# Shared-network products from fp32r parts in the mixing stage of a three-stage transformer kernel

## The chip, the cores and the metric

The kernel runs on one core of a Trainium2 chip. The metric is device time in microseconds of one execution of the whole program. A core has five engines with programs of their own that wait for each other through semaphores: TensorE (PE in the profile), VectorE (DVE), ScalarE (ACT), GpSimd (POOL) and SyncE (SP, which issues DMAs). Each engine executes its program strictly in the order in which it is written.

## The reference

Eight sequences of 512 tokens and 256 features go through attention, then each gets one class row in front (513 rows), then a linear recurrence and a mixture of experts:

```
h = attention(x)                                  # 16 heads
h = concat([cls, h], axis=1)                      # 513 rows a sequence
u = layernorm(h)
h = h + (C @ scan(Bu)) + D * u                    # state h_t = W h_{t-1} + B u_t, W circulant
u2 = layernorm(h)
shared = (silu(u2 @ Wg_s.T) * (u2 @ Wu_s.T)) @ Wd_s.T
probs = sigmoid(u2 @ Wr.T + rb); top 2 of 8 experts
out = h + shared + sum over the 2 experts of score * expert(u2)
```

Everything is fp32 at the interface.

## The kernel before

The program has four stages, each a block that ends for all engines together: the projections of q, k and v (`stage_qkv`), the attention (`stage_attention`), the mixing (`stage_mix`) and the experts (`stage_experts`). The change is in the mixing, with some placing of buffers in `program`.

The mixing goes through the eight batches (sequences) one after the other as a software pipeline written out by hand: every engine has a function `step(b, par, prev, this, nxt)`, called for b = 0 to 8. In step b an engine works on batch b (`this`), finishes the shared network of batch b - 1 (`prev`) and prepares batch b + 1 (`nxt`). Steps 1 to 6 run in a loop. There is no planner: the order of the lines is the order of the work.

TensorE's step: transposes of the normalised rows u (L1028); block 1 of the shared network of batch b - 1 (`shared_up`, L1058; a block m is a quarter of the 512 hidden features, its gate half and its up half); the product with m1 that makes the recurrence's input (L1096); block 2; transposes of the next attention heads; block 3; a small count for the experts' places (L1077, L1079); the product of the recurrence's result with m2 (L1040, `by_token`); the down products of batch b - 1 (L1066); transposes of u2; the output projection of batch b + 1 (L1040 too); the router's logits (L1127); block 0 of batch b. The operands of all of these are fp32.

VectorE's step: the choice of two experts for batch b - 1 (`top_two`, L733 to L742, and L1244); gate times up of blocks 0 and 1 (`shared_act`, L1186); then, when m1's product is made, four rotations (L1260 to L1263), two scans (L1264, L1266) and six operations to turn back (L1270 to L1276); gate times up of blocks 2 and 3; the rows' places in the experts' table (`place`, L1225 to L1231); sum and statistics of h2 (L1200 to L1208); normalising to u2 (L1214); the adds of the down products (L1191); sum and statistics of the next h (`first_sum`); the router's bias (L1313); normalising the next u. In step 0 there is also the work on the class rows (L1357 to L1370).

ScalarE copies transposes from PSUM (L963), computes the silu of each block (L959) and the sigmoid (L1002), and in steps 7 and 8 rounds expert weights to fp32r (`shorten_weights`, L770), which VectorE then subtracts from the weights to have the second part (`cut_weights`, L778).

GpSimd computes u times d and adds h (L909, L915), the power -1/2 of the variances (L903, `inverse_deviation`) and issues for each batch eight indirect DMAs that scatter row numbers and scores to the table (L930). SyncE loads the heads, stores u2 and h2, and loads one expert's weights a batch.

The expert stage already multiplies from two fp32r parts of both operands, through `split_products` (L72): short times short, short times rest, rest times short. An fp32 matmul of 128x512 shows as two records in the trace, an fp32r one as one.

## Time and profile before

| | us |
|---|---|
| median of 3 runs | 1290.72 |
| lowest, highest | 1283.68, 1291.52 |
| profiled execution | 1272.49 |
| its span | 1270.7 |
| its mean TensorE clock | 0.969 of full |
| PE busy in the span | 1168.8 (92%) |
| DVE busy | 828.0 (65%) |
| ACT busy | 496.1 (39%) |
| POOL busy | 394.5 (31%) |
| 600 to 700 us: PE, DVE, ACT, POOL busy | 95.39, 79.21, 22.55, 41.39 |

The profile is of one execution, so sums of durations stand against 1272.49, and the runs' median is 18 us above it. The stretch from 600 to 700 us lies wholly in the mixing stage, which begins at about 523 us with the class rows; its last down products run at 856 us, and the expert stage's first transposes start at 881.1. Busy shares do not say what an engine waits for; that is read from the waits and from the engines' instructions in order of time.

### The profile page before, as it was taken

To read this page: it belongs to the slowest core of one execution; us is meant where nothing else is said; L and a number is where in the kernel's file an instruction comes from. 1 tells how busy PE (TensorE), PEld (TensorE's weight loads), DVE (VectorE), ACT (ScalarE), POOL (GpSimd) and SP (SyncE) were. 2 spreads that over 40 slices of the span, in tenths; PEclk is the share of its full clock that TensorE was granted. 3 is DMA by queue.
4 is the path that set the end of the run, shared out by engine and by line. 5 is a ranking of instruction groups with operands and counts; after the bars stand their busy time and mean duration, and the time that the engine had idled before them with its cause. 6 is when DMAs were issued, how large, how long until landed. Compare 5 with 4: busy or idle time off the path is not lost. (4 is left out here: it accounts for less than half of the span.)

```text
span 1270.7 us, 21184 instructions
## 1 busy us (share of the span) xinstructions
PE 1168.8 (92%) x5606; PEld 699.3 (55%) x5607; DVE 828.0 (65%) x1463; ACT 496.1 (39%) x867; POOL 394.5 (31%) x515
## 2 busy tenths in 40 slices
PE   6996999999999999759999999982999999999997
PEld 3552233333333332445566665552888888888885
DVE  4998888888888885278777788884343333333432
ACT  2430677777777777421212121440222222222221
POOL 1021441011110111022443333452355544455543
PEclk9996899999999999889999999996999999999999
DMA  8885223333333321203444223311233333333332
GB/s 287 307 272 194 71 89 108 96 93 101 105 90 96 109 85 56 83 1 84 100 99 97 73 48 80 83 34 34 34 50 50 53 53 52 50 50 50 52 55 35
DMA packets 108675, 113.05 MB, mean 89 GB/s; under 512 B 26080, under 2 KB 97904, under 8 KB 107600
## 3 DMA queue, kind: packets, MB, share of 16 engines
q1 hardware_dynamic: 90528, 89.05, 24.4%
q0 software_dynamic: 18112, 23.57, 10.7%
q8 instruction: 17, 0.28, 0.1%
q14 instruction: 18, 0.15, 0.0%
HBM read 68.81 MB, written 43.62 MB: 88 GB/s over the span
## 5 line engine op out<-in xcount | busy, mean ns | idle before, releaser
L637 DVE TENSOR_REDUCE neg_max<-by_query 128x2 f32<-128x1024 f32 x256 | 301.7, 1220 | 62.8 <-PE by_query L538 62.1
L696 ACT ACTIVATE k_wu_e<-by_key 128x512 f32<-128x512 f32 x512 | 277.2, 601 | 83.5 <-PE by_key L546 80.1
L546 PE MATMUL by_key<-k_wg_e 99*128 99x512 bf16 x512 | 180.2, 386 | 2.6 <-ACT k_wu_e L696 2.1
L1455 POOL DMA_INDIRECT out_rows<-y,k_slot x72 | 113.9, 1583 | 189.8 <-DVE y L1583 175.2
L538 PE MATMUL by_query<-k_wg_e 96*128 96x512 bf16 x512 | 161.3, 398 | 11.6 <-PEq L106 7.5
L1543 ACT ACTIVATE gate<-ps_up 128x512 f32<-128x512 f32 x72 | 43.0, 598 | 321.8 <-PE ps_up L72 321.8
L1504 PE MATMUL ps_y<-k_wd_e,acts_T 128*128 x576 | 136.0, 379 | 0.8 <-ACT acts_T L1552 0.8
L557 PE MATMUL pv<-k_wu_e,k_wd_e 128*32 128x512 f32 x1024 | 136.2, 604 | 0.2 <-ACT k_wu_e L696 0.2
L72 PE MATMUL ps_up<-w_short,x_T 128*128 x288 | 133.5, 464 | 0.4 <-issue 0.4
L546 PEld LDWEIGHTS by_key<-k_wg_e 99*128 99x128 bf16 x512 | 42.1, 97 | 144.5 <-ACT k_wu_e L696 84.8
L1504 PEld LDWEIGHTS ps_y<-k_wd_e,acts_T 128*128 128x128 f32 x576 | 109.0, 189 | 18.0 <-issue 1.0
L72 PE MATMUL ps_up<-w_short,x_rest 128*128 x288 | 113.8, 395 | 0.0
L1567 DVE CAST x_T<-ps_x 128x256 fp32r<-128x256 f32 x72 | 30.6, 425 | 104.2 <-PE ps_x L1477 104.2
L538 PEld LDWEIGHTS by_query<-k_wg_e 96*128 96x128 bf16 x512 | 47.6, 100 | 85.6 <-DVE k_wd_e L651 13.2
L451 POOL CAST k_max_parts<-neg_max 128x16 bf16<-128x16 f32 x32 | 6.1, 190 | 283.7 <-PE by_key L546 244.9
L1583 DVE TENSOR_SCALAR y<-ps_y,k_slot 128x256 f32<-128x256 f32 x72 | 34.8, 484 | 77.9 <-DMA out_rows<-y,k_slot 64.1
L791 POOL DMA_INDIRECT k_x_in<-kept_x_rows,k_slot x72 | 70.7, 982 | 28.7 <-issue 21.1
L1576 DVE TENSOR_TENSOR acts<-gate,ps_up 128x512 f32<-128x512 f32 x72 | 49.6, 688 | 46.1 <-PE ps_up L72 46.1
L930 POOL DMA_INDIRECT kept_table<-k_pay,k_slot_i x64 | 67.1, 1049 | 23.5 <-issue 18.4
L206 PE MATMUL qk_ps<-k_wu_e,k_wqkv 128*128 128x512 f32 x128 | 57.8, 605 | 12.2 <-DMA k_wu_e<-in_xT 12.2
L903 POOL TENSOR_TENSOR mix_rstd<-mix_mv,k_minus_half 128x4 f32<-128x4 f32 x16 | 16.4, 1026 | 149.3 <-DVE mix_mv L1208 149.2
L1058 PE MATMUL mix_pairs<-k_mix_u_T,k_wg_s 128*128 128x512 f32 x128 | 61.3, 602 | 0.7 <-DVE mix_act_T L1186 0.6
(204 smaller groups left out, 1764.1 us busy)
## 6 DMA issues: line engine op xcount, KB each, us to landing
k_wg_e<-kept_qk SPq DMA_DIRECT2D x384, 64.0 KB, 2.1
kept_qk<-qk_parts SPq DMA_DIRECT2D x32, 384.0 KB, 3.4
kept_v<-v_ones SPq DMA_DIRECT2D x8, 1024.0 KB, 5.8
k_wd_e<-kept_v SPq DMA_DIRECT2D x32, 256.0 KB, 3.0
k_wu_e<-in_xT POOLq DMA_DIRECT2D x8, 512.0 KB, 4.4
kept_heads<-k_wd_e SPq DMA_DIRECT2D x8, 512.0 KB, 3.0
k_heads_in<-kept_heads SPq DMA_DIRECT2D x8, 512.0 KB, 11.3
k_wg_e<-in_wg_e SPq DMA_DIRECT2D x8, 512.0 KB, 6.7
```

The source lines that it names most:

```text
L72: mm = pe.matmul(out, short(lhs[a]), short(rhs[b]), start=(start and n == 0), stop=(stop and n == 2))
L206: mm = pe.matmul(qk_ps[:, j, :], wqkv[:, c, j * P:(j + 1) * P], xt[:, par, c, :], start=(c == 0), stop=(c == DC - 1))
L538: pe.matmul(by_query[:, pair_bank(b, g, k // 2) + k % 2, :], q_rows[0:KROWS, g, h, t * P:(t + 1) * P], k_rows[0:KROWS, g, h, :], start=Tru ...
L546: pe.matmul(by_key[:, key_bank(job), :], k_rows[0:SROWS, g, h, kt * P:(kt + 1) * P], q_rows[0:SROWS, g, h, :], start=True, stop=True).then ...
L557: mm = pe.matmul(pv[VW * h:VW * (h + 1), :], v_unit[:, g, kt, h, :], probs[:, G * (kt // 2) + h, kt % 2, :], start=(kt == 0), stop=(kt == ...
L637: dve.tensor_reduce(neg_max[:, g % 2, 2 * n:2 * n + 2], by_query[:, bank:bank + 2, :], AX.X, ALU.max, negate=True).then_inc(query_read, 1)
L696: act.activation(probs[:, key_tile(j) // 2 * G + j // 2 % G, j % 2, :], by_key[:, key_bank(job), :], ACT.Exp, scale=float(HD) ** -0.5).the ...
L791: pool.indirect_dma_start(out=mem["x_in"][:, r % FIRST_X, :], out_offset=None, in_=dram["x_rows"], in_offset=bass.IndirectOffsetOnAxis(ap= ...
L930: pool.indirect_dma_start(out=dram["table"], in_offset=None, in_=mem["pay"][:, t, n, :], out_offset=bass.IndirectOffsetOnAxis(ap=mem["slot ...
L1058: mm = pe.matmul(pairs[:, m % 2, n, :], w[:, c, m * P:(m + 1) * P], u2_T[:, c, :], start=(c == 0), stop=(c == DC - 1))
L1455: pool.indirect_dma_start(out=dram["out"], in_=y[:, r % 2, :], in_offset=None, compute_op=ALU.add, out_offset=bass.IndirectOffsetOnAxis(ap ...
L1504: mm = pe.matmul(ps_y[:, r % 2, 0:D], acts_T[:, m, :], mem["wd_e"][:, bass.ds(e, 1), m, :], start=(m == 0), stop=(m == FC - 1))
```

## The change

`shared_up` takes its products from two fp32r parts of the weights and of u2, three fp32r matmuls in place of one fp32. For that ScalarE makes a rounded copy of the transposes of u2 beside the plain one, and VectorE subtracts it (`u2_rest`) before it sums the next h; the shared weights are rounded on ScalarE at the stage's start and cut on VectorE in step 0 (`cut_shared`). Room is made by computing in place: state and result of the recurrence lie in u_T, gate times up in the gate, GpSimd's product in h2. Block 1 is made in two halves, one ahead of m1's product and one behind it. GpSimd waits for the choice of experts before its product, and computes the next batch's power before the last two scatters. The expert weights' rounding in the last steps is spread otherwise.

```diff
@@ stage_mix
+        state, hidden = u_T, u_T
+        u2_short = sb("mix_u2_short", [P, DC, S], FP32)
+        u2_rest = sb("mix_u2_rest", [P, DC, S], FP32)
+        wg_short, wu_short, wg_rest, wu_rest = (mem[n] for n in ("wg_short", "wu_short", "wg_left", "wu_left"))
...
-        act_T = sb("mix_act_T", [P, FC, S], FP32)
+        act_T = gate
@@ GpSimd
                     pool.wait_ge(ev["u_done"], b + 1)
-                    pool.tensor_tensor(ud[:, :, :], u[:, :, :], mem["d_row"]...
-                    pool.wait_ge(ev["ud_done"], 2 * b + 1)
                     if prev:
                         pool.wait_ge(ev["acc_stored"], 16 * (b - 1))
                         pool.wait_ge(ev["cls_stored"], 32)
-                    pool.tensor_tensor(h2[:, par, :, :], ud[:, :, :], h[:, :, :], ALU.add).then_inc(ev["ud_done"], 1)
+                        pool.wait_ge(ev["chosen_done"], b)
+                    pool.tensor_tensor(h2[:, par, :, :], u[:, :, :], mem["d_row"]...
+                    pool.wait_ge(ev["ud_done"], 2 * b + 1)
+                    pool.tensor_tensor(h2[:, par, :, :], h2[:, par, :, :], h[:, :, :], ALU.add).then_inc(ev["ud_done"], 1)
...
                     for t in range(TT):
+                        if t == TT - 1 and nxt:
+                            inverse_deviation(b + 1, 1)
+                            pool.sem_inc(ev["scatter_begun"])
                         for n in range(2):
                             pool.indirect_dma_start(
...
-                if nxt:
+                elif nxt:
                     inverse_deviation(b + 1, 1)
@@ ScalarE
             def silu(j, m):
                 act.wait_ge(ev["gate_made"], FC * j + m + 1)
-                act.wait_ge(ev["act_done"], FC * j)
+                act.wait_ge(ev["down_made"], 2 * j)
...
+            def shorten_turned(b):
+                act.wait_ge(ev["u2_turned"], b + 1)
+                act.activation(short(u2_short[:, :, :]), turn[:, :, :], ACT.Copy).then_inc(ev["u2_shortened"], 1)
...
                 if this:
                     copy_turned(u2_T, b, "u2_turned", "u2T_copied")
+                    shorten_turned(b)
...
-                    for n in range(8, 13):
+                    for n in (8, 9):
...
+            for to, w in ((wg_short, mem["wg_s"]), (wu_short, mem["wu_s"])):
+                act.activation(short(to[:, :, :]), w[:, :, :], ACT.Copy).then_inc(ev["shared_shortened"], 1)
@@ TensorE
-            def shared_up(j, m):
+            def shared_up(j, m, which=(0, 1)):
                 if m == 0:
                     pe.wait_ge(ev["acc_done"], 2 * j)
+                    pe.wait_ge(ev["u2_cut"], j + 1)
+                    pe.wait_ge(ev["shared_cut"], 2)
                 elif m >= 2:
                     pe.wait_ge(ev["act_done"], FC * j + m - 1)
-                for n, w in enumerate((mem["wg_s"], mem["wu_s"])):
+                for n in which:
+                    w_short, w_rest = ((wg_short, wg_rest), (wu_short, wu_rest))[n]
                     for c in range(DC):
-                        mm = pe.matmul(pairs[:, m % 2, n, :], w[:, c, m * P:(m + 1) * P], u2_T[:, c, :],
-                                       start=(c == 0), stop=(c == DC - 1))
-                mm.then_inc(ev["gate_made"], 1)
+                        mm = split_products(pe, pairs[:, m % 2, n, :],
+                                            (w_short[:, c, m * P:(m + 1) * P], w_rest[:, c, m * P:(m + 1) * P]),
+                                            (u2_short[:, c, :], u2_rest[:, c, :]), start=(c == 0), stop=(c == DC - 1))
+                if 1 in which:
+                    mm.then_inc(ev["gate_made"], 1)
...
-                    shared_up(b - 1, 1)
+                    shared_up(b - 1, 1, (0,) if this else (0, 1))
...                                                    # the product with m1 stands here
                 if prev:
+                    if this:
+                        shared_up(b - 1, 1, (1,))
                     shared_up(b - 1, 2)
...
                 if this:
                     pe.wait_ge(ev["u2T_copied"], b + 1)
+                    pe.wait_ge(ev["u2_shortened"], b + 1)
@@ VectorE
                 if prev:
                     shared_add(b - 1, 1 - par, 1)
-                else:
+                if this:
+                    dve.wait_ge(ev["u2_shortened"], b + 1)
+                    dve.wait_ge(ev["gate_made"], FC * b)
+                    dve.wait_ge(ev["u2T_copied"], b + 1)
+                    dve.tensor_tensor(short(u2_rest[:, :, :]), u2_T[:, :, :], u2_short[:, :, :],
+                                      ALU.subtract).then_inc(ev["u2_cut"], 1)
+                if not prev:
                     class_place()
                     class_add()
+                    cut_shared()
                 if nxt:
                     first_sum(b + 1)
...
+            def cut_shared():
+                dve.wait_ge(ev["cls_up"], 1)
+                for n, (to, part, w) in enumerate(((wg_rest, wg_short, mem["wg_s"]), (wu_rest, wu_short, mem["wu_s"]))):
+                    dve.wait_ge(ev["shared_shortened"], n + 1)
+                    dve.tensor_tensor(short(to[:, :, :]), w[:, :, :], part[:, :, :], ALU.subtract).then_inc(ev["shared_cut"], 1)
```

## Rows read from the trace of the kernel before

**Rows 1.** Waits of PE, 560 to 860 us: total us, times, longest.
```profile
PE mix_made L1040 <- DVE k_mix_hidden L1276: 9.4, 7, 2.1
PE mix_turn L1028 <- DVE k_mix_u L1214: 8.3, 7, 4.9
```

**Rows 2.** Timeline of PE in one batch: start, length, operation, idle time before.
```profile
655.67 1.09 PE L1028 MATMUL mix_turn<-k_ident,k_mix_u 128*128 128x128 f32 x8 [0.56 <-DVE k_mix_u L1214]
656.59 1.88 PE L1058 MATMUL mix_pairs<-k_mix_u_T,k_wg_s 128*128 128x512 f32 x4
...
660.03 3.60 PE L1096 MATMUL mix_made<-k_mix_u_T,k_m_T 128*128 128x512 f32 x8
...
673.22 3.72 PE L1040 MATMUL mix_made<-k_m_T,k_mix_hidden 128*128 128x256 f32 x16 [1.33 <-DVE k_mix_hidden L1276]
```

**Rows 3.** Timeline of PE, other batches: transposes of u, product with m2.
```profile
579.19 1.04 PE L1028 MATMUL mix_turn<-k_ident,k_mix_u 128*128 128x128 f32 x8
...
694.00 1.09 PE L1028 MATMUL mix_turn<-k_ident,k_mix_u 128*128 128x128 f32 x8 [0.61 <-DVE k_mix_u L1214]
...
710.90 3.72 PE L1040 MATMUL mix_made<-k_m_T,k_mix_hidden 128*128 128x256 f32 x16 [1.08 <-DVE k_mix_hidden L1276]
...
806.99 1.09 PE L1028 MATMUL mix_turn<-k_ident,k_mix_u 128*128 128x128 f32 x8 [0.49 <-DVE k_mix_u L1214]
```

**Rows 4.** Timeline of DVE in the same batches.
```profile
655.66 2.36 DVE L734 TENSOR_TENSOR k_eq<-mix_probs,k_best 128x32 f32<-128x32 f32 x1
...
663.03 1.28 DVE L1186 TENSOR_TENSOR mix_act_T<-mix_gate,mix_pairs 128x512 f32<-128x512 f32 x2
664.23 0.68 DVE L1260 TENSOR_TENSOR k_x_in<-mix_made,k_cos 128x512 f32<-128x512 f32 x1
...
676.68 0.69 DVE L1200 TENSOR_TENSOR mix_h<-mix_made,mix_h 128x512 f32<-128x512 f32 x1
...
680.11 0.17 DVE L1208 TENSOR_SCALAR mix_mv<-mix_mv 128x4 f32<-128x4 f32 x1
...
702.00 0.69 DVE L1260 TENSOR_TENSOR k_x_in<-mix_made,k_cos 128x512 f32<-128x512 f32 x1 [1.42 <-PE mix_made L1096]
```

**Rows 5.** Timeline of ACT, one silu and one copy of transposes.
```profile
660.23 0.60 ACT L959 ACTIVATE mix_gate<-mix_pairs 128x512 f32<-128x512 f32 x1 [2.41 <-PE mix_pairs L1058]
...
684.75 1.02 ACT L963 ACTIVATE k_mix_u_T<-mix_turn 128x1024 f32<-128x1024 f32 x1 [12.34 <-PE mix_turn L1028]
```

**Rows 6.** Timeline of POOL: the product with d, the power.
```profile
655.61 2.35 POOL L909 TENSOR_TENSOR k_mix_ud<-k_mix_u,k_d_row 128x1024 f32<-128x1024 f32 x1 [1.50 <-DVE k_mix_u L1214]
...
691.49 1.04 POOL L903 TENSOR_TENSOR mix_rstd<-mix_mv,k_minus_half 128x4 f32<-128x4 f32 x1
```

**Rows 7.** Timeline of PE in the expert stage, around six fp32r matmuls of 512 columns.
```profile
1001.36 0.58 PE L72 MATMUL ps_up<-w_short,x_T 128*128 x1
...
1002.92 0.60 PE L1497 MATMUL ps_a<-k_ident,acts 128*128 128x128 f32 x4
```

**Rows 8.** Timelines of PE (first two), DVE and ACT: idle times, and step 0.
```profile
557.29 5.69 PE L1040 MATMUL mix_made<-k_m_T,k_mix_hidden 128*128 128x256 f32 x16 [6.46 <-DVE k_mix_hidden L1276]
...
856.69 7.17 PE L1066 MATMUL mix_pairs<-k_wd_s,mix_act_T 128*128 128x256 f32 x32 [3.02 <-DVE mix_act_T L1186]
...
567.77 0.17 DVE L1357 COPY k_pos<-k_slot 128x8 f32<-128x8 f32 x1
...
570.65 0.41 DVE L1370 TENSOR_TENSOR k_cls_h<-k_cls_h,mix_pairs 128x256 f32<-128x256 f32 x1
...
569.73 1.02 ACT L963 ACTIVATE k_mix_u_T<-mix_turn 128x1024 f32<-128x1024 f32 x1 [17.83 <-PE mix_turn L1028]
```

**Rows 9.** Timelines of ACT and DVE at the end of the stage.
```profile
836.07 1.02 ACT L963 ACTIVATE k_mix_u_T<-mix_turn 128x1024 f32<-128x1024 f32 x1 [2.94 <-PE mix_turn L1028]
...
836.94 1.22 DVE L778 TENSOR_TENSOR wu_rest<-k_wu_e,w_short 128x1024 fp32r<-128x1024 f32 x1
...
845.97 0.19 DVE L1225 TENSOR_TENSOR k_pos<-mix_turn,k_next_slot 128x32 f32<-128x32 f32 x1 [0.84 <-DMA kept_table<-k_pay,k_slot_i]
```

More of the change, by code:

```diff
@@ L115, in stage_qkv @@
         fold_ps = pb("fold_ps", [P, 2, S], FP32)
-        b_w, c_T = mem["mix_ud"][:, 0:2, :], mem["mix_ud"][:, 2:4, :]
+        b_w, c_T = mem["mix_u2"][:, 0:2, :], mem["mix_u2"][:, 2:4, :]
         to_planes, from_planes = mem["mix_u"][:, 0:2, :], mem["mix_u"][:, 2:4, :]
@@ L802, in stage_mix @@
         heads = mem["heads_in"]
-        h, u, ud, u2 = (mem["mix_" + n] for n in ("h", "u", "ud", "u2"))
+        h, u, u2 = (mem["mix_" + n] for n in ("h", "u", "u2"))
         by_feature = "p (c t) n -> p c (t n)"
-        heads_T, u_T, state, hidden, u2_T = (mem["mix_" + n][:, :, :].rearrange(by_feature, c=DC)
-                                             for n in ("heads_T", "u_T", "state", "hidden", "u2_T"))
+        heads_T, u_T, u2_T = (mem["mix_" + n][:, :, :].rearrange(by_feature, c=DC) for n in ("heads_T", "u_T", "u2_T"))
+        state, hidden = u_T, u_T
+        u2_short = sb("mix_u2_short", [P, DC, S], FP32)
+        u2_rest = sb("mix_u2_rest", [P, DC, S], FP32)
+        wg_short, wu_short, wg_rest, wu_rest = (mem[n] for n in ("wg_short", "wu_short", "wg_left", "wu_left"))
         h2 = sb("mix_h2", [P, 2, TT, D], FP32)
@@ L836, in stage_mix @@
                  "logits_biased sigmoid chosen_done counts_made counts_read slots_ready slots_out "
-                 "gate_made gate_done act_done down_made acc_done u2_stored "
+                 "gate_made gate_done act_done down_made acc_done u2_stored u2_shortened u2_cut shared_shortened shared_cut "
                  "cls_stats cls_pow cls_u cls_turned cls_copied cls_y cls_h2 cls_logits cls_biased cls_sigmoid "
@@ L968, in class_copy @@
                 act.activation(to, cls_ps[bank][:, 0:D].rearrange("p (c n) -> p c n", c=2), ACT.Copy).then_inc(ev["cls_copied"], 1)
+            def shorten_turned(b):
+                act.wait_ge(ev["u2_turned"], b + 1)
+                act.activation(short(u2_short[:, :, :]), turn[:, :, :], ACT.Copy).then_inc(ev["u2_shortened"], 1)
             def step(b, par, prev, this, nxt):
                 if this:
+                    act.wait_ge(ev["y_made"], 2 * b)
                     copy_turned(u_T, b, "u_turned", "uT_copied")
@@ L981, in step @@
                     shorten_weights(act, mem, 3)
+                if not this:
+                    act.wait_ge(ev["u2_stored"], 16 * B)
+                    act.wait_ge(ev["logits_made"], B)
+                    for n in (10, 11):
+                        shorten_weights(act, mem, n)
                 if prev:
@@ L984, in step @@
                 if last:
-                    act.wait_ge(ev["bu_made"], B)
                     act.wait_ge(ev["ud_done"], 2 * B)
@@ L1004, in step @@
                 if not this:
-                    act.wait_ge(ev["u2_stored"], 16 * B)
-                    act.wait_ge(ev["logits_made"], B)
-                    for n in (13, 14, 15):
+                    act.wait_ge(ev["gate_made"], FC * B)
+                    for n in range(12, 16):
                         shorten_weights(act, mem, n)
+            for to, w in ((wg_short, mem["wg_s"]), (wu_short, mem["wu_s"])):
+                act.activation(short(to[:, :, :]), w[:, :, :], ACT.Copy).then_inc(ev["shared_shortened"], 1)
             class_copy(0, cls_u_T, 0)
@@ L1263, in step @@
                     scan(dve.tensor_tensor(back[3], made[:, 0, :], sin, ALU.mult))
+                    dve.wait_ge(ev["y_made"], 2 * b)
                     scan(dve.tensor_tensor_scan(state[:, 0, :], back[0], back[1], mem["state0"][:, 0:1],
@@ L1712, in program @@
         kinds.update((name, (shape, dtype)) for name, shape, dtype in others)
-        for name in ("heads_in", "mix_heads_T", "mix_h", "mix_u_T", "mix_ud", "mix_state", "mix_hidden", "mix_u", "mix_u2",
-                     "mix_u2_T"):
+        kinds["wg_short"] = kinds["wu_short"] = kinds["wg_s"]
+        for name in ("heads_in", "mix_heads_T", "mix_h", "mix_u_T", "mix_u", "mix_u2", "mix_u2_T"):
             kinds[name] = ([P, TT, D], FP32)
-        order = ("heads_in", "mix_heads_T", "mix_h", "mix_u_T", "mix_ud", "mix_state", "mix_hidden", "bo_row", "d_row", "wo_T",
-                 "m1_T", "m2_T", "mix_u", "cos", "sin", "mix_u2", "mix_u2_T")
+        order = ("heads_in", "mix_heads_T", "mix_h", "mix_u", "bo_row", "d_row", "wo_T", "cos", "sin", "mix_u_T",
+                 "m1_T", "m2_T", "mix_u2", "mix_u2_T", "wg_short", "wu_short", "wg_s", "wu_s", "wr_T", "rb_row")
         for name in order + tuple(name for name in kinds if name not in order):
+            if name == "wg_s":
+                with ExitStack() as alias:
+                    for left in ("wg_left", "wu_left"):
+                        mem[left] = alias.enter_context(nc.sbuf_tensor("k_" + left, *kinds[name]))
             if name not in mem:
```

6 lines of the change are left out of this document (2 added, 4 removed).

## Prediction

> **What bounds the kernel now.** I read the busy shares by stretch first: the change touches only the mixing stage (about 523 to 865 us). There TensorE is busy 95% of the time and VectorE near 79%, which looks like a TensorE bound, and the change makes TensorE's work shorter. So I looked next at what ends TensorE's few idle times: they end with VectorE every time, once at the scan's result, once at the normalised rows [rows 1]. Then I laid one batch side by side on all engines, from the transposes of u (call this T) to those of the next batch. The reader should see two halves.
>
> First half, T to the product with m2: TensorE waits 1.33 us in one batch and 1.08 in another [rows 2, 3] for VectorE, whose work from its first rotation to the end takes 673.22 - 664.23 = 8.99 us [rows 2, 4]. What matters is when that work starts. It is T + 8.56 where VectorE comes late (664.23 against 655.67 [rows 2, 4]), because small operations of the top-two choice stand still beside GpSimd's product: 2.36 us for 128x32 elements, from 655.66, beside GpSimd's 2.35 from 655.61 [rows 4, 6]. It is T + 8.00 in the other batch, and there VectorE sat idle 1.42 us until m1's product was made [rows 3, 4]. The two halves of the stage's products with the shared weights fill the time around it.
>
> Second half, product with m2 to the next T: 694.00 - 673.22 = 20.78 us [rows 2, 3]: m2's product, the down products, transposes of u2, the projection, then VectorE's sum and statistics, GpSimd's power at 691.49, normalising. The power ends last: GpSimd had issued eight scatters first. Mean period: (806.99 - 579.19) / 6 = 37.97 us [rows 3], so the first half is 17.2 us in the mean.
>
> **The change part by part, steady batches.**
> *Products of the shared network.* One block m has four fp32 products of 512 columns: 656.59 to 660.03, 3.44 us [rows 2]. After, twelve fp32r ones. The expert stage runs six of this shape in 1002.92 - 1001.36 = 1.56 us [rows 7], so at most 3.12, and less for the second six, whose first matmul has no switch before it: I take 2.93. TensorE is given 0.3 to 0.5 us a block, 1.3 to 2 us a batch. None of these blocks stands between m2's product and the next T save the last one (block 0 of the next), and that one already ends before the normalised rows come [rows 1]. In the first half they stand ahead of a wait for VectorE. So this gain turns into waiting, unless the start of VectorE's work comes earlier.
>
> *It comes later.* Block 1 is cut in two: gate half ahead of m1's product, up half behind it. The semaphore that releases the silu and the product gate x up of block 1 is set by the up half alone, and in VectorE's program that product still stands ahead of the wait for m1's product. So the rotations start after: transposes 0.92, gate half 1.56, m1's product 3.60, up half 1.56, silu 0.60 and its release 0.05, gate x up 0.64 (1.28 for two) [rows 2, 4, 5, 7]: T + 8.93. Plus 8.99 is T + 17.92, against 17.2: +0.7 a batch. The freed contention (GpSimd now waits for the choice) takes top-two's stalls away, but it ends in this wait.
>
> Here a rule of the Trainium skill speaks for the change (SBUF — State Buffer, Who interferes with whom): a VectorE instruction with two SBUF inputs and a GpSimd one that reads SBUF block each other entirely. The trace agrees, 2.36 beside 2.35. If the freed time counted in full, the batches that pay it would be about 2 us faster.
>
> By rows it is worth at most 8.56 - 8.00 = 0.56 in every other batch, and nothing with the new wait ahead.
>
> *The second part of u2.* ScalarE writes a second copy of the transposes (1.02, as the first, which starts at 684.75 [rows 5]), ready at 686.8. VectorE subtracts: 128x1024, 1.14 to 1.22 us [rows 9], to 688.0, and only then may it sum the next h. Sum and statistics back to back take 676.68 to 680.28, 3.60 us [rows 4], so they end at 691.6; the power, freed of the last two scatters by the new order, starts at 691.65 instead of 691.49 [rows 6]: +0.2. Without the new order GpSimd would be no later, so that move pays nothing. The last two scatters move behind the power; behind them waits only GpSimd's own product, which now waits for the choice anyway. The choice is made at T + 7.4 with both stalls (663.03 [rows 4]) and 2 to 4 us earlier without them, so GpSimd's two products, some 5 us, end by about T + 10, ahead of VectorE's two-input scans at T + 11.3 (8.93 and four rotations). SP's queue keeps its order.
>
> Sum of a steady batch: +0.9, six of them: **+5.4 us**. Last batch's first half: **+0.4**.
>
> **Step 0 pays most.** There VectorE's cut stands *ahead* of the class rows' work. ScalarE's copy starts at 569.73 [rows 8], second copy ends 571.8, cut to 572.95. VectorE had started the class placing at 567.77 and the class sum at 570.65 [rows 8]; these 2.9 and 0.35 us now end at 576.2, two cuts of the shared weights (1.14 each [rows 9]) at 578.5, sum and statistics (3.60) at 582.1, then power and normalising as in a steady batch, 694.00 - 691.49 = 2.5 us, plus 0.1: T of batch 1 at 584.8 instead of 579.19 [rows 3]. **+5.6 us.** TensorE idles about 3 us twice before it. It ran slow after an idle time of 6.46 us (5.69 us for sixteen matmuls that take 3.72 [rows 2, 8]) and at full speed after one of 3.02 [rows 8]; from 0 to 2 us for this, I take **+1**.
>
> **The end.** In the last batch the cut waits for two copies from 836.07 [rows 9]: 838.1, cut 839.3, two expert cuts 841.5, where they had ended at 838.2 with 0.98 idle behind them: the choice shifts by 2.4. Of that shift, VectorE's idle time ahead of gate x up and of the placing takes up half. Placing, which had waited 0.84 us for the scatters of the batch before and began at 845.97 [rows 9], then begins at 847.2: **+1.2**. Behind it wait eight scatters, the table, the gathers and the expert stage. TensorE's faster blocks lie beside this.
>
> *Nothing for:* the two shortenings of shared weights at ScalarE's start (1.05 each; covered by ScalarE's idle time before the class copies; at most 2 us if that cover were gone); waits on m2's product of the batch before, long past; buffers in place. ScalarE's spread of expert shortenings lies under the scatters.
>
> **Sum:** 5.4 + 0.4 + 5.6 + 1.0 + 1.2 = 13.6 us. The profiled execution took 1272.5 us (span 1270.7), so 1286.1 for it. The runs' median is 1290.7, 18 us above; the added time is the same, so I forecast **1304.3**. Bounds of the case: steady 3 to 8, step 0 with clock 4.5 to 8, end 0.5 to 2.5: +8 to +18.5, 1299 to 1309.
>
> **Rivals.**
> A. *TensorE's clock falls in the new gaps.* TensorE would have ended its first half at T + 14.4 to 15.1 and wait until 17.9: 2.8 to 3.5 us idle in each batch. For it: the fall after 6.46 us; against: none after 3.02 [rows 8]. Price 5.69 - 3.72 = 1.97 in up to seven batches: 13.8 more, 1318. It decides if these gaps act as the long one did and not as the short one.
>
> The Trainium skill warns of this (TensorE: Matmul & The Clock Gate, Loop structure matters more than you think): idle waits between bursts of matmuls send the clock down. By it the sum would be 1318; the trace bears it out for the long gap only.
>
> B. *TensorE stays the bound, not slower.* If VectorE's start isn't held by block 1 (it decides at T + 8.0), TensorE's 0.5 us for each of 32 blocks counts: -16, and 0.56 in half the batches, -2; step 0 takes 5.6 back: -12, 1279. For it: 95% busy. Against: every wait of TensorE ends with VectorE [rows 1], and the order in VectorE's program.
>
> C. *Milder.* Step 0's overlap is better than I laid it (the class work finds its inputs earlier), or steady batches lose only 0.2: +3 to +8, 1294 to 1299.
>
> D. *The split isn't faster with weights as the stationary part*: if each of twelve cost the 0.58 us of a single record [rows 7], a block would be 7.0, TensorE's first half would end near T + 27 instead of 17.9, seven times 9 more: 1367. Against: the expert stage streams the same shapes at 1.56 for six [rows 7].
>
> **Chances.** Forecast 0.60, A 0.13, B 0.09, C 0.14, D 0.04. The predicted time is the forecast's. The range 1288 to 1320 takes in the forecast, C and A, and leaves out most of B and D. A measurement of this kernel tells about 1% (12.9 us) from no change: slower means above 1303.6. Somewhat over half of the forecast lies there, with A and D: 0.50. Faster is below 1277.8, a part of B: 0.08. Within: 0.42.
>
> **What would show it.** In the changed profile: gate x up of block 1 ends just before the first rotation, about T + 8.9, and TensorE's wait for the scan's result grows from 1.2 to about 3 us a batch; the period grows from 38.0 to 38.9; in step 0, ScalarE's copy of u2 to T of batch 1 takes 15 us instead of 9.5 [rows 3, 8]; top-two has no 2.3 us operation. I am wrong if rotations start before T + 8.2, if the period falls, or if m2's product takes over 5 us (rival A).

## The result and the profile after

The changed kernel took 1300.87 us (median of 4 runs, 1298.18 to 1304.03), the kernel before 1287.21 us (4 runs beside them, 1283.68 to 1291.52): ratio 1.0106 [1.0054, 1.0157], 13.7 us more. The forecast was 13.6 us more, 1304.3. That agreement is partly luck. In a later comparison, with more runs, the same pair gave 1297.56 against 1278.53: 1.016 [1.0137, 1.0182], 19 to 20 us more. And the two profiled executions, on which all steps below are read, lie 31.2 us apart (span 1301.9 against 1270.7): the one of before was faster than all its timed runs. So the steps are judged one by one.

The page after: TensorE is busy longer, though its work was made shorter, and its granted clock over the span fell from 0.969 to 0.947.

```profile
span 1301.9 us, 21479 instructions
PE 1174.1 (90%) x5734; PEld 739.1 (57%) x5735; DVE 816.6 (63%) x1473; ACT 505.6 (39%) x877; POOL 397.9 (31%) x515
```

TensorE's waits from 560 to 860 us (total, times, longest). Those for the scan's result (first line) answer to 9.4 us in [rows 1], those for the normalised rows to 8.3.

```profile
PE mix_made L1060 <- DVE k_mix_u_T L1303: 32.8, 8, 6.3
PE mix_turn L1048 <- DVE k_mix_u L1241: 15.1, 8, 4.9
```

TensorE in one batch after, its timeline (start, length, operation, idle time before), with the next T. The answer to [rows 2].

```profile
588.49 1.09 PE L1048 MATMUL mix_turn<-k_ident,k_mix_u 128*128 128x128 f32 x8 [0.65 <-DVE k_mix_u L1241]
589.33 0.48 PE L72 MATMUL mix_pairs<-mix_u_short,k_wg_short 128*128 128x512 f32 x1
...
590.81 3.59 PE L1121 MATMUL mix_made<-k_mix_u_T,k_m_T 128*128 128x512 f32 x8
...
593.84 0.79 PE L72 MATMUL mix_pairs<-mix_u_short,k_wu_short 128*128 128x512 f32 x1
...
606.12 6.69 PE L1060 MATMUL mix_made<-k_m_T,k_mix_u_T 128*128 128x256 f32 x16 [3.75 <-DVE k_mix_u_T L1303]
...
630.13 1.09 PE L1048 MATMUL mix_turn<-k_ident,k_mix_u 128*128 128x128 f32 x8 [1.51 <-DVE k_mix_u L1241]
```

Two things differ from before. TensorE stands idle 3.75 us ahead of m2's product instead of 1.33, as predicted; and the product, the same sixteen matmuls, takes 6.69 us instead of 3.72. Its granted clock is in the windows of this stretch (columns: us, busy time and instructions of PE, PEld, DVE, ACT, POOL, then the clock, DMA share, GB/s):

```profile
588.50:602.00 13.50, 13.50 (x60) 9.79 (x60) 8.56 (x22) 3.25 (x4) 4.82 (x2) 1.00 0.17 44
602.00:606.10 4.10, 0.37 (x7) 0.19 (x5) 4.03 (x8) 0.60 (x1) 0.00 (x0) 0.91 0.02 6
606.10:609.50 3.40, 3.38 (x8) 2.75 (x9) 3.06 (x14) 0.00 (x0) 0.00 (x0) 0.50 0.00 0
609.50:612.80 3.30, 3.30 (x10) 2.66 (x10) 1.51 (x4) 0.00 (x0) 0.00 (x0) 0.60 0.00 0
612.80:620.00 7.20, 7.20 (x38) 6.33 (x37) 4.36 (x14) 0.00 (x0) 3.97 (x4) 1.00 0.06 20
```

Full (2.4 GHz) until the idle time, half (1.2 GHz) from near its end through most of the product, full again for the down products. The product's lengths in the batches after are 6.69, 6.41, 6.13, 5.41, 6.31, 6.22 and, last batch, 6.14. So this was rival A's mechanism, in every batch.

VectorE and GpSimd in the same batch (timeline):

```profile
588.48 0.19 DVE L734 TENSOR_TENSOR k_eq<-mix_probs,k_best 128x32 f32<-128x32 f32 x1
...
591.64 2.41 POOL L918 TENSOR_TENSOR mix_h<-k_mix_u,k_d_row 128x1024 f32<-128x1024 f32 x1 [4.78 <-DVE mix_chosen L1271]
...
595.91 0.60 ACT L968 ACTIVATE mix_gate<-mix_pairs 128x512 f32<-128x512 f32 x1 [5.27 <-PE mix_pairs L72]
...
596.54 0.69 DVE L1213 TENSOR_TENSOR mix_gate<-mix_gate,mix_pairs 128x512 f32<-128x512 f32 x1 [4.36 <-ACT mix_gate L968]
...
597.14 0.68 DVE L1287 TENSOR_TENSOR k_x_in<-mix_made,k_cos 128x512 f32<-128x512 f32 x1
```

The top-two operation of 2.36 us in [rows 4] is 0.19 here: the order of GpSimd did free VectorE. But VectorE then stands idle 4.36 us for the silu of block 1, and the rotations start at 597.14 = T + 8.65, though m1's product had ended at 594.4.

**Where the 31.2 us of the two profiles lie.** 2.2 before the stage (its first class transposes start at 527.46 against 525.23; the change touches nothing there). 7.1 in step 0 (T of batch 1 at 588.49 against 579.19, less those 2.2). 19.2 in six batches: the last T is 835.48, so a period of 41.17 against 37.97, of which the slower product is 2.5 in the mean. 2.7 behind that T.

### The profile page after: what moved, and what is told of

Its sections match the earlier page's. It is cut to its first block and busy times, and to the rows that moved or that the text cites. A ratio compares the mean times of both kernels' runs of the same rounds, so it can differ in the third digit from the quotient of the medians.

```text
span 1301.9 us, 21479 instructions
## 1 busy us (share of the span) xinstructions
PE 1174.1 (90%) x5734; PEld 739.1 (57%) x5735; DVE 816.6 (63%) x1473; ACT 505.6 (39%) x877; POOL 397.9 (31%) x515
## 5 line engine op out<-in xcount | busy, mean ns | idle before, releaser
L1060 PE MATMUL mix_made<-k_m_T,k_mix_u_T 128*128 128x256 f32 x128 | 48.4, 560 | 32.8 <-DVE k_mix_u_T L1303 32.8
L939 POOL DMA_INDIRECT kept_table<-k_pay,k_slot_i x64 | 69.0, 1078 | 24.4 <-issue 16.3
```

The lines of the kernel that those rows point to most:

```text
L939: pool.indirect_dma_start(out=dram["table"], in_offset=None, in_=mem["pay"][:, t, n, :], out_offset=bass.IndirectOffsetOnAxis(ap=mem["slot ...
```

## The experiments

| run | median us | before beside it | ratio |
|---|---|---|---|
| the changed kernel | 1297.56 | 1278.53 | 1.016 [1.0137, 1.0182] |
| the kernel before, again | 1278.48 | 1276.73 | 1.0006 [0.999, 1.0022] |
| E1 products back in fp32 | 1300.83 | 1276.98 | 1.0174 [1.0145, 1.0203] |
| E2 gate x up of block 1 later | 1273.36 | 1276.98 | 0.9974 [0.9955, 0.9993] |
| E3 class rows first | 1294.53 | 1276.98 | 1.0138 [1.0109, 1.0166] |
| E4 gap filled | 1289.49 | 1276.98 | 1.0095 [1.0072, 1.0118] |
| E5 GpSimd's order alone | 1270.65 | 1278.53 | 0.9963 [0.9945, 0.9981] |
| E6 block 1 whole | 1283.38 | 1278.53 | 1.0045 [1.0025, 1.0065] |
| E7 = E2 + E3 + cut from PSUM | 1279.0 | 1278.53 | 1.000 [0.9983, 1.0017] |
| E8 = E7 + store first | 1277.97 | 1287.89 | 0.9918 [0.9892, 0.9944] |
| E9 = E8 + gap filled | 1278.2 | 1287.89 | 0.9923 [0.9897, 0.9948] |
| E10 = E8 in fp32 | 1279.97 | 1287.89 | 0.9941 [0.9916, 0.9965] |

The ratio is not always that of the two medians beside it (the changed kernel, E5, E8): it comes with the interval, and is the one to go by. Runs with the same time of before (1276.98, 1278.53, 1287.89) shared a chip, so times are set side by side within such a group, and ratios across groups. "Period" is a sixth of the time from the first T to the last.

### E4, the gap filled: what does the clock alone cost?

> The changed kernel with three more fp32 matmuls of 512 columns (0.86 us each, their result is thrown away) after the count in each of batches 1 to 6, so that TensorE works through 2.6 of the 3.6 us ahead of m2's product. Work is added and none taken away. Theory G: m2's product 3.7 us in these batches instead of 6.1 to 6.7, period 38.6 to 38.9, total 13 to 16 us below the changed kernel. Rival S: no difference, or a little slower.

```diff
                     if this:
                         count(b - 1, nxt)
+                        if nxt:
+                            for _ in range(3):
+                                pe.matmul(turn[:, 0, :], ident[:, :], mem["cos"][:, 1:T1], start=True, stop=True)
```

Three more fp32 matmuls stand in the idle time, their result unused. The batch of E4 on TensorE, and its clock around the product (windows):

```profile
588.21 1.09 PE L1048 MATMUL mix_turn<-k_ident,k_mix_u 128*128 128x128 f32 x8 [1.57 <-DVE k_mix_u L1244]
...
605.87 3.72 PE L1060 MATMUL mix_made<-k_m_T,k_mix_u_T 128*128 128x256 f32 x16 [1.08 <-DVE k_mix_u_T L1306]
...
626.90 1.09 PE L1048 MATMUL mix_turn<-k_ident,k_mix_u 128*128 128x128 f32 x8 [1.51 <-DVE k_mix_u L1244]
```

```profile
602.00:605.80 3.80, 2.78 (x11) 0.99 (x7) 3.77 (x7) 0.60 (x1) 0.00 (x0) 1.00 0.01 2
605.80:609.50 3.70, 3.63 (x17) 3.22 (x18) 3.34 (x16) 0.00 (x0) 0.00 (x0) 1.00 0.00 0
```

T to m2's product is 17.66 us, as in the changed kernel, so VectorE is where it was. But the product is back at 3.72, in all six batches, and the period is 38.64. More work on TensorE made the kernel about 8 us faster than the changed one, if the ratios of two chips are set side by side (1.0095 against 1.016; E1, on E4's chip, stood at 1.0174). The product and the period came out as expected; the whole gained less than the 13 to 16 us. This shows that the clock's fall comes from the idle time and what it costs. It also comes close to the forecast's own world, the change without a fall: +0.7 a batch where 0.9 was forecast, 1.0095, or 12.1 us, where 13.6 was. Only the last batch, which has no filling, still fell (5.41 behind 4.46 idle).

### E1, products in fp32: is it the faster product that costs?

> The changed kernel with the shared network's products in plain fp32 again, everything else (second copy of u2, its cut, the split of block 1, GpSimd's order) left as changed. The products then take more time, so the idle time ahead of m2's product shrinks from 3.6 us to under 2. Theory G (the clock falls in that gap, and m2's product then takes 6.3 us instead of 3.7): m2's product back at 3.7, period 38.9 to 39.3 us instead of 41.2, whole time 14 to 18 us below the changed kernel although its matmuls are slower. Rival S (only VectorE's later start and the cut cost time, the clock does not matter to the total): the same as the changed kernel or up to 5 us above it.

```diff
-                        mm = split_products(pe, pairs[:, m % 2, n, :],
-                                            (w_short[:, c, m * P:(m + 1) * P], w_rest[:, c, m * P:(m + 1) * P]),
-                                            (u2_short[:, c, :], u2_rest[:, c, :]), start=(c == 0), stop=(c == DC - 1))
+                        mm = pe.matmul(pairs[:, m % 2, n, :], (mem["wg_s"], mem["wu_s"])[n][:, c, m * P:(m + 1) * P],
+                                       u2_T[:, c, :], start=(c == 0), stop=(c == DC - 1))
```

The cuts and copies stay, their results unused (the cuts of the shared weights write in place); two shortenings of expert weights move later. I had expected the longer matmuls to shorten the gap and so to keep the clock. They shortened it, to 2.3 to 2.5 us in six batches and 3.2 in the last, and the clock fell all the same, in all seven:

```profile
608.56 5.41 PE L1058 MATMUL mix_made<-k_m_T,k_mix_u_T 128*128 128x256 f32 x16 [2.48 <-DVE k_mix_u_T L1300]
```

E1 was no faster than the changed kernel. My expectation of it failed; what follows is that the gain of fp32r on TensorE is wholly lost in the changed order, and that a gap of 2.3 to 2.5 us is already too long here (E6 has gaps of this length behind which the clock held).

### E2, gate x up later: does block 1 hold the rotations?

> The changed kernel with VectorE's product gate x up of block 1 moved behind the four rotations. Rotations then wait for m1's product alone and start near T + 5.5 instead of T + 8.65; m2's product near T + 15.1 instead of T + 17.6; TensorE's idle time ahead of it about 1.3 us instead of 3.6. Theory G: m2's product 3.7 us, period about 36.1 us, total 33 to 37 us below the changed kernel. Rival S: 2.5 us a batch from the start alone, m2's product as long as it was, total 15 to 18 us below.

```diff
-                    shared_act(b - 1, 1)
                     if not this:
+                        shared_act(b - 1, 1)
...
                     scan(dve.tensor_tensor(back[3], made[:, 0, :], sin, ALU.mult))
+                    if prev:
+                        shared_act(b - 1, 1)
                     dve.wait_ge(ev["y_made"], 2 * b)
```

One VectorE instruction moves behind four. Timeline of VectorE and TensorE in E2:

```profile
589.85 1.09 PE L1048 MATMUL mix_turn<-k_ident,k_mix_u 128*128 128x128 f32 x8 [1.53 <-DVE k_mix_u L1241]
...
595.80 0.69 DVE L1287 TENSOR_TENSOR k_x_in<-mix_made,k_cos 128x512 f32<-128x512 f32 x1 [2.27 <-PE mix_made L1121]
...
598.41 0.69 DVE L1213 TENSOR_TENSOR mix_gate<-mix_gate,mix_pairs 128x512 f32<-128x512 f32 x1
...
605.38 3.72 PE L1060 MATMUL mix_made<-k_m_T,k_mix_u_T 128*128 128x256 f32 x16 [1.65 <-DVE k_mix_u_T L1305]
...
626.42 1.09 PE L1048 MATMUL mix_turn<-k_ident,k_mix_u 128*128 128x128 f32 x8 [1.50 <-DVE k_mix_u L1241]
```

The rotations start at T + 5.95 and wait for m1's product alone; T to m2's product is 15.5, the gap 1.65, the clock stays up, and the period is 36.62, below that of before. The kernel is 0.26% faster than before, where the changed one was 1.6% slower. This shows the step "it comes later" at its cause. Of the 4.5 us a batch between the first profile of the changed kernel (41.17) and 36.62, 2.5 are the clock and 2.0 the earlier product (T + 17.58 to T + 15.56). The whole gain lay between the two expectations: by the ratios (1.016 against 0.9974) some 24 us, where theory G had 33 to 37 and rival S 15 to 18. The product at 3.72 is G's.

### E6, block 1 whole

> The changed kernel with block 1 whole ahead of m1's product, as before. m1's product is made near T + 7.3 and gate x up of block 1 is long done by then, so rotations start at T + 7.3 instead of 8.65 and m2's product at T + 16.3 instead of 17.6, TensorE's idle time ahead of it 2.4 us instead of 3.6. Theory G with the fall seen after 2.3 to 2.5 us: m2's product 5.4, period about 39.2, 12 us below the changed kernel (8 to 15). Rival S (start alone): 1.3 us a batch, 8 to 10 us below with m2's product as long as in the changed kernel; if the split is what helps, slower than the changed kernel.

```diff
-                    shared_up(b - 1, 1, (0,) if this else (0, 1))
+                    shared_up(b - 1, 1)
...
-                    if this:
-                        shared_up(b - 1, 1, (1,))
                     shared_up(b - 1, 2)
```

Both halves ahead of m1's product: the product comes later, but block 1 no longer ends behind it. T to m2's product falls to 16.3, the gap to 2.4; the product takes 5.41 and 5.39, then four times 3.72. Period 37.92 against 40.36 for the changed kernel on the same chip, 14 us less in all. The cut of block 1 into halves was thus a dear choice, though the place of gate x up was dearer (E2: some 24 us). Behind the same gap the clock fell in two batches and held in four (timeline of TensorE, the first batch and the third):

```profile
601.99 5.41 PE L1060 MATMUL mix_made<-k_m_T,k_mix_u_T 128*128 128x256 f32 x16 [2.45 <-DVE k_mix_u_T L1301]
...
680.14 3.72 PE L1060 MATMUL mix_made<-k_m_T,k_mix_u_T 128*128 128x256 f32 x16 [2.44 <-DVE k_mix_u_T L1301]
```

### E3, class rows first: what does step 0 pay?

> The changed kernel with, in step 0, the class rows' placing and sum and the cuts of the shared weights ahead of the cut of u2. VectorE no longer idles 4 us while ScalarE makes the second copy, so T of batch 1 comes about 4 us earlier; the steady batches stay at 41.2 us. Theory: total 4 us below the changed kernel (2 to 5). Rival (the idle time only moves to the first waits of batch 1): no difference.

```diff
+                if not prev:
+                    class_place()
+                    class_add()
+                    cut_shared()
                 if this:
                     dve.wait_ge(ev["u2_shortened"], b + 1)
...
-                if not prev:
-                    class_place()
-                    class_add()
-                    cut_shared()
```

ScalarE's copy of u2 to T of batch 1, in step 0 of the changed kernel and of E3 (timelines):

```profile
573.55 1.02 ACT L972 ACTIVATE k_mix_u_T<-mix_turn 128x1024 f32<-128x1024 f32 x1 [17.32 <-PE mix_turn L1048]
...
576.66 0.17 DVE L1397 COPY k_pos<-k_slot 128x8 f32<-128x8 f32 x1
```

```profile
569.01 0.17 DVE L1397 COPY k_pos<-k_slot 128x8 f32<-128x8 f32 x1
...
570.92 1.02 ACT L972 ACTIVATE k_mix_u_T<-mix_turn 128x1024 f32<-128x1024 f32 x1 [17.77 <-PE mix_turn L1048]
...
581.96 1.09 PE L1048 MATMUL mix_turn<-k_ident,k_mix_u 128*128 128x128 f32 x8 [2.00 <-DVE k_mix_u L1241]
```

In the changed kernel the class placing (L1397) starts behind the cut, 3.1 us after the copy's start, and T comes 588.49 - 573.55 = 14.94 after it. With the class rows first they fill VectorE's idle time ahead of the copy, and it is 11.04. So 3.9 of the 5.5 us came from the order of VectorE's program, as laid out. In whole runs that gain is not settled: E3's 1.0138 and the changed kernel's 1.016 were taken on two chips, and their intervals overlap.

### E5, GpSimd's order alone, on the kernel before

> The kernel before with GpSimd's new order alone (its product waits for the choice; the power ahead of the last two scatters). Theory: top-two has no stalled operation, rotations start at T + 8.0 in every batch instead of 8.0 to 8.6, the power no longer waits for scatters, so the period falls from 37.97 to 37.2 to 37.5: 3 to 5 us faster than before. Rival (the prediction's view that this move pays nothing without the rest): within 2 us of before.

```diff
                     pool.wait_ge(ev["u_done"], b + 1)
+                    if prev:
+                        pool.wait_ge(ev["chosen_done"], b)
...
                     for t in range(TT):
+                        if t == TT - 1 and nxt:
+                            inverse_deviation(b + 1, 1)
+                            pool.sem_inc(ev["scatter_begun"])
...
-                if nxt:
+                elif nxt:
                     inverse_deviation(b + 1, 1)
```

Faster than before: 0.9963, period 36.90. Timeline of E5 from T:

```profile
618.95 0.19 DVE L734 TENSOR_TENSOR k_eq<-mix_probs,k_best 128x32 f32<-128x32 f32 x1
...
619.05 1.04 PE L1033 MATMUL mix_turn<-k_ident,k_mix_u 128*128 128x128 f32 x8
...
622.20 2.35 POOL L911 TENSOR_TENSOR k_mix_ud<-k_mix_u,k_d_row 128x1024 f32<-128x1024 f32 x1 [2.20 <-DVE mix_chosen L1249]
...
635.89 3.72 PE L1045 MATMUL mix_made<-k_m_T,k_mix_hidden 128*128 128x256 f32 x16 [1.08 <-DVE k_mix_hidden L1281]
...
653.19 1.04 POOL L903 TENSOR_TENSOR mix_rstd<-mix_mv,k_minus_half 128x4 f32<-128x4 f32 x1 [1.67 <-DVE mix_mv L1213]
```

T to m2's product is 16.84 to 16.94, some 0.3 less than the mean before (no stall beside GpSimd's product). The power starts 17.30 us after m2's product, where it was 18.27 in [rows 2, 6], as six scatters stand ahead of it and not eight; TensorE no longer waits at T at all. So GpSimd's order is worth 1.05 us a batch by itself, 6 in all by the traces and 4.7 by the ratio. In the changed kernel ScalarE's second copy and the cut of u2 stand ahead of the sum that the power waits for, and the second half is no shorter than before (E2: 21.04 us).

### E7 to E10, the parts put together

> The changed kernel with gate x up of block 1 behind the rotations, the class work first in step 0, and the second part of u2 cut straight from the transposes in PSUM as soon as the rounded copy is there (ScalarE rounds first, the plain copy comes after the cut). Against the kernel with the first of these alone: the cut ends 1 us earlier, so the period falls from 36.6 to 35.6, and step 0 loses 4 us: 9 to 12 us below it, 1262 to 1266, ratio to before 0.988 to 0.991. Rival (the cut is hidden behind the projection anyway): period 36.6, 1269.

```diff
-                    dve.wait_ge(ev["u2T_copied"], b + 1)
-                    dve.tensor_tensor(short(u2_rest[:, :, :]), u2_T[:, :, :], u2_short[:, :, :],
+                    dve.tensor_tensor(short(u2_rest[:, :, :]), turn[:, :, :], u2_short[:, :, :],
...
-                    copy_turned(u2_T, b, "u2_turned", "u2T_copied")
                     shorten_turned(b)
+                    act.wait_ge(ev["u2_cut"], b + 1)
+                    copy_turned(u2_T, b, "u2_turned", "u2T_copied")
```

The cut reads the transposes in PSUM, so it waits for one copy and not for two. Two batches took the expected 35.6 us, but the mean was 37.0 and the kernel level with before, not 9 to 12 us below E2. GpSimd's first product, now in place in the buffer of the sum rows, must wait until the rows stored from it have gone out, and its second then falls beside a scan (timelines of GpSimd and VectorE in E7):

```profile
695.48 2.44 POOL L918 TENSOR_TENSOR mix_h<-k_mix_u,k_d_row 128x1024 f32<-128x1024 f32 x1 [5.00 <-DMA out_rows<-mix_h]
697.99 2.40 POOL L921 TENSOR_TENSOR mix_h<-mix_h,k_mix_h 128x1024 f32<-128x1024 f32 x1
698.58 2.90 DVE L1295 TENSOR_TENSOR_SCAN k_mix_u_T<-k_x_in,k_state 128x512 f32<-128x512 f32 x1
```

The scan took 2.90 instead of 1.28, ended 1.1 us behind GpSimd's product, and the gap on TensorE behind it was 3.26. The wait is the changed kernel's own, not only E7's (GpSimd's waits, 560 to 860 us, second run of the changed kernel, then E7):

```profile
POOL mix_h L918 <- DMA out_rows<-mix_h: 17.4, 4, 6.3
```

```profile
POOL mix_h L918 <- DMA out_rows<-mix_h: 25.6, 6, 5.7
```

> The combined kernel with SyncE's store of the finished sums issued ahead of the load of the next expert's weights instead of behind it. In the combined kernel GpSimd's products waited for that store (25.6 us in all) and ran into VectorE's scans (2.90 us instead of 1.28), so that rotations to m2's product took up to 11.2 us instead of 9.7. Theory: no such wait, the product with m2 15.5 us after T in every batch, idle time ahead of it 1.65, m2's product 3.7 in nearly all, period 35.6: 1262 to 1268. Rival (the clock falls at random whatever the store does): 1273 to 1279 as the combined kernel.

```diff
             def step(b, par, prev, this, nxt):
...
+                if this and prev:
+                    store_sum(b, par)
                 if nxt:
                     load_expert(b + 1)
...
-                if prev:
-                    sp.wait_ge(ev["acc_done"], 2 * b)
-                    sp.dma_start(out_rows[bass.ds(T1 * b - T1 + 1, S), :].rearrange("(t p) n -> p t n", p=P),
-                                 h2[:, 1 - par, :, :]).then_inc(ev["acc_stored"], 16)
+                if prev and not this:
+                    store_sum(b, par)
```

The store is issued ahead of the next expert's loads on SP's queue. GpSimd's wait is gone, T to m2's product is 15.5 to 15.6 in all batches but one, and this is the best ratio measured: 0.9918. In time its 1277.97 is not the lowest: the kernel before took some 10 us more here than beside the other experiments, and there is no trace of it from this chip. In the one batch the clock fell ahead of T, and the transposes and the first products of block 1 paid (T to m2's product 17.14; timeline of TensorE):

```profile
620.74 1.71 PE L1054 MATMUL mix_turn<-k_ident,k_mix_u 128*128 128x128 f32 x8 [1.92 <-DVE k_mix_u L1247]
```

The expectation of 1262 to 1268 us failed. The period is 37.6, not 35.6: VectorE stands idle ahead of the second half of the projection's sum (timeline of E8), although TensorE had begun the logits behind that projection at 652.90.

```profile
652.90 1.95 PE L1161 MATMUL mix_turn<-k_wr_T,k_mix_u_T 128*128 128x8 f32 x16
...
654.72 0.69 DVE L1233 TENSOR_TENSOR k_mix_h<-mix_made,k_bo_row 128x512 f32<-128x512 f32 x1 [1.55 <-remote]
```

What it waits for there the trace doesn't say. The idle time, 1.55 to 1.72 us, stands in all six steps of the loop in E8, E9 and E10 and in none of E7; these three have the store first, and they also shared a chip, with none of the other experiments on it. Which of the two brings it stays open.

> The same with one more fp32 matmul of 512 columns (0.86 us, result thrown away) behind the count in batches 1 to 6. Theory G: the remaining idle time is 0.8 us, the clock never falls there, 0 to 6 us below the kernel without it, with less spread. Rival: no difference where the clock no longer falls; never slower, since TensorE waits there anyway.

```diff
+                        for _ in range(1 if nxt else 0):
+                            pe.matmul(turn[:, 0, :], ident[:, :], mem["cos"][:, 1:T1], start=True, stop=True)
```

The gap falls from 1.65 to 0.69 and nothing changes (0.9923): at 1.65 the clock had already held.

> The kernel with the store first, with the shared network's products in plain fp32. It tells what the fp32r products are worth once VectorE's start, step 0, the cut and the store no longer cover them. TensorE's work of a batch is then 36.85 us as in the kernel with GpSimd's order alone, so the period is 36.9 to 37.2 against 35.6: 8 to 10 us slower than with fp32r. Rival (TensorE is no bound even here): the same time.

The edit is that of E1, on E8. TensorE doesn't wait for the scan in the steady batches, the period is 37.7, and the ratio 0.9941 overlaps E8's. So even here the fp32r products are worth 2 to 3 us where 8 to 10 were expected, and that difference isn't settled: the steady batches differ by 0.1 us each (37.62 against 37.70), and two shortenings of expert weights moved later too.

### The two kernels once more

> The changed kernel as it is, beside the others on one chip, because its first ratio (1.011) stands against runs of the kernel before that were 10 us slower than the 13 seen since (median 1277). Theory G: m2's product 5.4 to 6.7 us in nearly every batch, against 3.7 before; time 1295 to 1301, ratio 1.015 to 1.019. Rival (the first ratio was right and the earlier profile unlucky): ratio 1.008 to 1.012, with m2's product at 3.7 in most batches.

Period 40.36; the product with m2 took 5.41, 5.41, 5.41, 6.34, 3.72, 5.12 and 5.41. So the fall is there in a second execution, with a smaller price. In one batch GpSimd's late product lay beside a scan (2.28 us) and pushed T to m2's product to 18.51.

> The kernel before, once more, for a second trace of it. The runs of it beside the experiments had medians of 1277 to 1288 us, its first trace 1272.5. Theory (the clock also falls now and then in its own gaps, 1.1 to 1.3 us ahead of m2's product, or around step 0 and the last batch): the new trace is longer by 4 to 12 us, its extra time lies in m2's products or project products that take 5.4 us instead of 3.7, and the steady batches without a fall are 38.0 us as before. Rival (the difference lies outside the mixing stage, or in all of it alike): batches as before, and stage borders moved.

The profile of before used ahead of the prediction was a lucky execution. In this one the steady batches are the same (period 37.95, product 3.72, clock 1.00), but step 0 ran at the lower clock for longer, and the last batch's product fell (timeline of TensorE):

```profile
560.71 6.74 PE L1040 MATMUL mix_made<-k_m_T,k_mix_hidden 128*128 128x256 f32 x16 [6.33 <-DVE k_mix_hidden L1276]
...
828.89 5.41 PE L1040 MATMUL mix_made<-k_m_T,k_mix_hidden 128*128 128x256 f32 x16 [1.96 <-DVE k_mix_hidden L1276]
```

Its span is 7.2 us longer (1277.9). So some 7 of the 31 us between the first two profiles are no part of the change. Why the median of before differs between comparisons (1276.7 to 1287.9) was not settled.

## Why the prediction was right, and where it wasn't

**The direction and its cause were right.** VectorE, not TensorE, decides; the faster products turn into waiting; gate x up of block 1 holds the rotations. Predicted start T + 8.93, measured T + 8.65; predicted T to m2's product 17.92, measured 17.58 in the mean of six batches. The twelve matmuls of a block took 2.80 us (block 2, 595.62 to 598.42, at a spacing of 0.23), where 2.93 was taken. E2 shows the cause by removing it. The first half grew by less than forecast, though: 0.35 us against 17.2 before, where 0.7 was taken. Rivals B and D are out, and C (3 to 8 us more) did not show either: E4, free of the fall in the six batches, stood at 12.1.

**Step 0 was right in size.** Predicted 15 us from copy to T, measured 14.94 (14.93 in the second profile); predicted 5.6 more, 5.5 of them found. (The prediction's own terms from 572.95 on end at 584.7, not 584.8: 5.5.) The rest of its 7.1 is m1's product at the lower clock (5.40 against 3.70), for which 1 was taken; the second profile of before shows the same (5.35), so that part belongs to the execution and not to the change. Between the second profiles step 0 grew by only 2.1, as there before had both products slow (5.35 and 6.74) and the changed kernel one (5.73). One gap of about 3 us did bring a fall: the twelve products of block 0 ran at the lower clock (0.50), but T waited for VectorE anyway (timeline of TensorE, m1's product and the first of block 0):

```profile
547.18 5.40 PE L1121 MATMUL mix_made<-k_mix_u_T,k_m_T 128*128 128x512 f32 x8 [2.04 <-ACT k_mix_u_T L972]
...
582.38 0.76 PE L72 MATMUL mix_pairs<-mix_u_short,k_wg_short 128*128 128x512 f32 x1 [3.12 <-DVE k_wu_left L1358]
```

**The end cost less than forecast, but for the clock.** 2.7 us more from the last T on, of which 2.4 is m2's product at the lower clock (6.14). That leaves under 0.3 for what was forecast at 1.6: the first half of the last batch did not grow (852.99 - 835.48 = 17.51, before 824.53 - 806.99 = 17.54).

**The step that failed is the steady batch: +0.9 forecast, +3.2 measured** (2.4 between the second profiles, 40.36 against 37.95). The prediction computed the gap of 2.8 to 3.5 us (measured 3.6 to 3.8) and then costed it at nothing, on one row: no fall after 3.02 us [rows 8]. Further rows of before spoke the same way (1.33 and 1.08, and 2.11 in the last batch, no fall), but a few rows that went well are no bound, and the same trace had a row that speaks against them: at the class rows, behind 3.77 us idle, TensorE ran at half the clock for 5 us, though it had been full up to the gap (timeline and clock of before):

```profile
525.23 0.69 PE L1141 MATMUL mix_pairs<-k_ident,mix_h 128*128 128x128 f32 x2 [3.77 <-DVE mix_h L1328]
...
824.53 3.72 PE L1040 MATMUL mix_made<-k_m_T,k_mix_hidden 128*128 128x256 f32 x16 [2.11 <-DVE k_mix_hidden L1276]
```

```profile
525.20:530.70 5.50, 4.53 (x14) 3.47 (x15) 1.02 (x3) 0.77 (x2) 0.00 (x0) 0.51 0.73 261
```

Rival A had the mechanism, at a chance of 0.13 and a price of 1.97 a time; measured 1.4 to 3.0, in 7 of 7 and 6 of 7 batches. The prediction had named m2's product over 5 us as a sign of being wrong, and by that sign it was. The Trainium skill (TensorE: Matmul & The Clock Gate, Loop structure matters more than you think) names long waits between matmuls as what makes TensorE run slow; its example is a wait for a DMA. The traces agree: 6.69 behind 3.75 idle, 3.72 behind 1.08 in E4.

**Why the sum agreed nevertheless.** It was 13.6 against 13.7 because the first comparison of medians gave less than the later one, by the ratio 20. E4, without the fall in the six batches, gave 12.1. The fall's share in them is then some 8 us of 20 by the ratios, and 15 of 31 in the first pair of profiles. A term of the size of the fall was missing, and a first measurement on the low side hid it: that is luck.

**"That move pays nothing" holds only with the cut.** E5 shows 1.05 us a batch for GpSimd's order alone. With the cut the second half grew by 0.3 without the clock (E2: 21.04 against 20.78), about as forecast (0.2).

**One collision was missed.** The prediction let GpSimd's products end at T + 10, ahead of the scans. In the batch shown of the first profile they do (596.5, T + 8.0), but where the store comes late they don't, and a scan pays 1.0 us (the changed kernel again) or 1.6 us (E7). The wait was there to be seen in the diff: the product is made in place in the rows that SP stores.

## What to carry to other kernels

Make an operation faster only after asking who releases the engine that waits behind it; here the release of a chain on VectorE moved later, and all of TensorE's gain turned into idle time. Then price the idle time itself: compute the gap, look for every gap in the trace and what followed it, outside the changed stretch too (here 3.77 us at the class rows), and let a gap longer than those that are known to be harmless carry a large chance of a slower engine. And try the side changes alone: the order of GpSimd, by itself on the kernel before (E5), beat the whole change.

## What the runs showed of the hardware

The clock fell in the idle time and the next 16 matmuls (m2's product) paid for it. Their length was 3.72 us at the full clock, and 5.1 to 6.8 after a fall. By idle time ahead of them:

| idle us | where (profiles, where more than one) | fell |
|---|---|---|
| up to 1.66 | before (2), E2, E4, E5, E7, E8, E9, E10 | never |
| 1.93 to 2.11 | E7 (2); last batch of before (2) and E5 | 2 of 5 |
| 2.31 to 2.48 | E1, E6; last batch of E8, E9 | 10 of 14 |
| 2.76 to 3.26 | E7 (2); last batch of E1, E2 | 3 of 4 |
| 3.57 to 3.77 | changed (2), E3 | 15 of 17 |
| 4.33 to 4.58 | one batch or two of changed (2), E3, E4, E6, E7 | 7 of 7 |
| 6.33 to 6.47 | step 0 of all 14 | 14 of 14 |

So there is a range, from about 1.9 to 3.8 us, in which the same gap may or may not bring the fall: in E3 and in the second run of the changed kernel one batch each kept 3.72, behind 3.58 and 3.75. What decides between them the runs don't show.

Other matmuls pay as well: at the class rows of both first profiles TensorE ran at half the clock behind 3.76 and 3.77 us idle, in E8 the transposes behind 1.92 us idle took 1.71 us instead of 1.09, and in step 0 of the changed kernel the products of block 0 ran at half the clock behind 3.12.

A VectorE scan with two inputs from SBUF beside GpSimd's 128x1024 product took 2.90 us instead of 1.28.
